# Product order in the gated experts, biases among the sends, linear attention in two phases, and routers' normalisations without turned tokens

## The reference, cut to what matters

```python
# the mixtures of experts (L0, L1, L3, each used twice): a router picks 2 of 8 experts (L1: 1, by capacity)
logits = x @ router_w.T (+ router_b)            # [4096, 8]
# L3 has gated experts with biases
h1, h2 = split(x @ w1[e].T + b1[e], 2)          # 2 x 512
out_e  = (silu(h1) * h2) @ w2[e].T + b2[e]
y      = sum over the 2 chosen e of weight_e * out_e

# L0_attn_b, linear attention, 16 heads of 8, two key/value sets
q, k_i = unit(silu(x @ Wq) + 0.5), unit(silu(x @ Wk[i]) + 0.5)   # unit: divided by each head's norm
state  = product over i of (k_i.T @ v_i / SEQ), per head
y      = (groupnorm(q @ state) * g + b) @ Wo + bo
```

## Time and profile before

| | us |
|---|---|
| median of 3 runs (lowest, highest) | 6225.26 (6223.73, 6227.15) |
| the profiled execution's own time | 6223.72 |
| its span | 6221.8 |
| PE / PEld / DVE busy | 3906.2 (63%) / 2459.3 (40%) / 3758.3 (60%) |
| ACT / POOL busy | 2448.4 (39%) / 1708.2 (27%) |

### The profile page before, as it was taken

One profiled execution on the slowest core, in us unless ns is written; L12 is line 12 of the kernel. 1 busy time (PEld: TensorE's weight loads), 2 busy tenths in 40 slices (PEclk: granted clock), 3 DMA queues, 4 the chain that ended last, 5 costly groups with the idle time before them and its releaser, 6 DMA issues. The chain is left out here.

```text
span 6221.8 us, 78605 instructions
## 1 busy us (share of the span) xinstructions
PE 3906.2 (63%) x21844; PEld 2459.3 (40%) x21844; DVE 3758.3 (60%) x6990; ACT 2448.4 (39%) x4474; POOL 1708.2 (27%) x1709
## 2 busy tenths in 40 slices
PE   5756648466664488724666664688855847476474
PEld 3546438222233233322222223344434636454464
DVE  4323651599974677544888886655567635566354
ACT  2334226355532277613545443233333524243242
POOL 0043014355542355422333340000001140301412
PEclk8868659688876699856778785799966779887898
DMA  2012003100001222012000000000000011100111
GB/s 82 0 55 75 1 10 91 41 1 0 0 4 54 74 82 89 22 36 79 0 1 0 0 0 2 18 1 0 0 2 2 2 45 41 39 8 2 45 42 51
DMA packets 224866, 170.50 MB, mean 27 GB/s; under 512 B 27435, under 2 KB 211602, under 8 KB 223714
## 3 DMA queue, kind: packets, MB, share of 16 engines
q1 hardware_dynamic: 204130, 125.44, 6.8%
q0 software_dynamic: 20480, 41.98, 2.3%
HBM read 92.02 MB, written 74.45 MB: 27 GB/s over the span
## 5 line engine op out<-in xcount | busy, mean ns | idle before, releaser
L1775 POOL TENSOR_TENSOR XN<-s_l_attn_a_h,LOG 128x512 f32<-128x512 f32 x512 | 642.5, 1276 | 768.6 <-DVE s_l_attn_a_h L1815 753.5
L1815 DVE TENSOR_TENSOR_SCAN s_l_attn_a_h<-s_l_attn_a_da,XN 128x512 f32<-128x512 f32 x512 | 598.5, 1211 | 142.9 <-ACT s_l_attn_a_da L1760 102.7
L1751 PE MATMUL s_l_attn_a_y_ps<-XN,c_ident 128*128 128x512 f32 x1024 | 588.7, 704 | 25.2 <-DVE s_l_attn_a_y L2027 15.4
L1760 ACT ACTIVATE s_l_attn_a_da<-s_l_attn_a_delta,s_l_attn_a_a 128x510 f32<-128x510 f32 x512 | 353.3, 690 | 526.0 <-DVE s_l_attn_a_h L1815 525.5
L483 DVE COPY s_l_ffn_ffn_xt<-s_l_ffn_ffn_turned 128x128 f32<-128x128 f32 x416 | 120.9, 292 | 711.1 <-PE s_l_ffn_ffn_turned L604 709.5
L569 POOL DMA_INDIRECT s_l_ffn_ffn_back<-slots_y,s_l_ffn_ffn_slots x320 | 302.8, 946 | 875.3 <-DMA slots_y<-PICK 566.4
L623 PE MATMUL s_l_ffn_ffn_down<-down,s_l_ffn_ffn_hid 128*128 x2944 | 421.1, 284 | 193.4 <-DVE s_l_ffn_ffn_hid L496 186.0
L623 PEld LDWEIGHTS s_l_ffn_ffn_down<-down,s_l_ffn_ffn_hid 128*128 128x128 f32 x2944 | 361.2, 192 | 233.6 <-issue 228.5
L416 ACT COPY s_l_ffn_ffn_own_w<-up 128x512 f32 (+2 forms) x416 | 305.0, 734 | 375.4 <-DVE s_l_ffn_ffn_expert_no L467 277.3
L1730 PE MATMUL s_l_attn_a_spread<-s_l_attn_a_parts,s_l_attn_a_pick 96*128 96x512 bf16 x512 | 182.2, 443 | 390.3 <-DVE XN L1806 243.2
L561 POOL DMA_INDIRECT slots_x<-XN,s_l_ffn_ffn_slots x320 | 311.5, 973 | 388.9 <-DVE s_l_ffn_ffn_slots L460 293.2
(11 more groups left out here) (631 smaller groups left out, 8651.3 us busy)
## 6 DMA issues: line engine op xcount, KB each, us to landing
XNT<-slots_x SPq DMA_DIRECT2D x32, 640.0 KB, 6.3
slots_y<-LOG SPq DMA_DIRECT2D x16, 640.0 KB, 4.3
slots_y<-PICK SPq DMA_DIRECT2D x16, 640.0 KB, 4.3
s_l_attn_b_qr<-s_l_attn_b_q_rows SPq DMA_DIRECT2D x64, 144.0 KB
s_l_attn_b_kr<-s_l_attn_b_k_rows SPq DMA_DIRECT2D x64, 144.0 KB
XNT<-slots_x SPq DMA_DIRECT2D x8, 768.0 KB, 7.0
slots_x<-PICK SPq DMA_DIRECT2D x10, 512.0 KB, 6.4
slots_x<-XN,s_l_ffn_ffn_slots POOLq DMA_INDIRECT x320, 2.2
```

The lines of the kernel that those rows point to most:

```text
L1751: last = self.nc.tensor.matmul(self.y_ps[:, i, :], self.k.ident[:], self.hc[n % 2][:, i, :], start=(n == 0), stop=(n == NST - 1))
L1760: self.nc.scalar.activation(self.da[:, i, :, 1:], self.delta[par][:, i, :].rearrange("p (b t) -> p b t", b=BPG)[:, :, 1:], ACT.Exp, scale= ...
L1775: self.nc.gpsimd.tensor_tensor(self.hc[n % 2][:, i, :], self.h[n % 2][:, i, :], self.c_rows[n % 2], ALU.mult).then_inc(self.hc_ready, 1)
L1815: self.nc.vector.tensor_tensor_scan(self.h[n % 2][:, i, :], self.da[:, i, :, :].rearrange("p b t -> p (b t)"), self.u[n % 2][:, i, :], 0.0 ...
```

## The change

Four edits, in the order of the file.

1. `layer_norm` gets `keep_cols`. The six normalisations of routers pass False: ScalarE then writes only `cols`, and TensorE waits for that copy on `turned_free`.
2. In `sparse_experts`, where gated, the work of `expert_bias` (which is gone) joins the block: GpSimd's product first of all, TensorE's turns and products between the ranks and the experts, VectorE's adds behind the gates. The four PSUM buffers of the up products serve for it; `ranks` shares two of them, hence `slots_used`.
3. In the loop over tiles, `gate_hid(j - 1)` stands ahead of `shift(j)`.
4. `l0_attn_b` runs in two phases: a turn of the loop does the first half (projection to state) of one pair of units and the second half (q times state to x) of the pair before. The projections of both units share one set of PSUM banks. It takes no statistics any more, so the next normalisation does.

```diff
@@ layer_norm
-                        pe.wait_ge(cols_ready, g + (i + 1))
+                        if keep_cols:
+                            pe.wait_ge(cols_ready, g + (i + 1))
+                        else:
+                            pe.wait_ge(turned_free, g + (i + 3))
...
-                        nc.scalar.copy(cols[i][:], turned[i][:]).then_inc(cols_ready, 1)
-                    nc.scalar.copy(xnt, turned[i][:]).then_inc(turned_free, 1)
+                        copied = nc.scalar.copy(cols[i][:], turned[i][:])
+                        copied.then_inc(cols_ready if keep_cols else turned_free, 1)
+                    if keep_cols:
+                        nc.scalar.copy(xnt, turned[i][:]).then_inc(turned_free, 1)
@@ sparse_experts, vector
+            if gated:
+                dve.sem_inc(slots_used, 1)
...
             dve.drain()
+            if gated:
+                for g in range(GROUPS):
+                    dve.wait_ge(bias_up, g + 1)
+                    xg = k.X[:, g * GT:(g + 1) * GT, :]
+                    nc.vector.tensor_tensor(xg, xg, bias_ps[g % 4], ALU.add).then_inc(bias_added, 1)
+                dve.drain()
             for j in range(min(2, NT)):
                 take_xt(j)
             for j in range(NT):
                 if j + 2 < NT:
                     take_xt(j + 2)
                 if gated:
-                    shift(j)
                     if j > 0:
                         gate_hid(j - 1)
+                    shift(j)
@@ sparse_experts, scalar
+                act.wait_ge(gates_up, 1)
+                for h in range(2):
+                    last = nc.scalar.copy(gates_t[:, h, :], turned[h][:])
+                last.then_inc(gates_turned, 1)
@@ sparse_experts, gpsimd
+            if gated:
+                nc.gpsimd.tensor_tensor(spread[:],
...
+                                        ALU.mult).then_inc(spread_ready, 1)
             pool.wait_ge(slots_ready, 1)
@@ sparse_experts, tensor, behind the ranks
+                for h in range(2):
+                    last = nc.tensor.transpose(turned[h][:], k.GATE[:, h * HT:(h + 1) * HT, :].rearrange("p t e -> p (t e)"), k.ident[:])
+                last.then_inc(gates_up, 1)
+                pe.wait_ge(gates_turned, 1)
+                pe.wait_ge(spread_ready, 1)
+                pe.wait_ge(slots_used, 1)
+                for g in range(GROUPS):
+                    if g >= 4:
+                        pe.wait_ge(bias_added, g - 3)
+                    h, q = divmod(g * GT, HT)
+                    nc.tensor.matmul(bias_ps[g % 4], gates_t[:, h, :], spread[:, q:q + GT, :], start=True, stop=True).then_inc(bias_up, 1)
+                pe.wait_ge(bias_added, GROUPS)
             pe.wait_ge(experts_ready, 1)
@@ l0_attn_b
-        proj = s.two_ps("proj", [P, TPB, 4 * D])
+        proj, proj_v = s.ps("proj", [P, TPB, 4 * D]), s.ps("proj_v", [P, TPB, 2 * D])
...
+            step(0, None)
+            with engine.Fori(0, PAIRS - 1) as pair:
+                step(pair * 2 + 2, pair * 2)
+            step(None, BATCH - 2)
...
+            # tensor, step(a, b): a is the newer pair, b the older
+                if a is not None:
+                    project(a, 0)
+                if b is not None:
+                    take_from_state(b, 0)
+                    take_from_state(b + 1, 1)
+                if a is not None:
+                    project(a + 1, 1)
+                if b is not None:
+                    turn_out(b, 0)
+                    turn_out(b + 1, 1)
+                    project_out(b, 0)
+                    project_out(b + 1, 1)
+                if a is not None:
+                    turn_and_add_up(a, 0)
+                    turn_and_add_up(a + 1, 1)
```

More of the change, by code:

```diff
@@ L649, in l0_ffn @@
         consts, loads = sparse_consts(nc, k, s)
-        layer_norm(nc, k, name + "_ln", k.bufs["L0_ffn_router"], 8, keep_rows=True, loads=loads)
+        layer_norm(nc, k, name + "_ln", k.bufs["L0_ffn_router"], 8, keep_rows=True, loads=loads, keep_cols=False)
         softmax8(nc, k, name + "_gate", False)
         sparse_experts(nc, k, name + "_ffn", consts, 2, 4, 4)
[L655 to L699, removed]
@@ L1006, in l0_attn_b @@
     HD = 8
-    BPG = 1
+    PAIRS = BATCH // 2
     with Scope(nc, name) as s:
@@ new lines, in project, with take_from_state @@
+            def project(u, m):
+                pe.wait_ge(xg_ready, u + 1)
+                since(pe, biased, u)
+                for t in range(TPB):
+                    xt = xg[m][:, t * P:(t + 1) * P]
+                    nc.tensor.matmul(proj[:, t, :], xt, w["L0b_w"][:, 0:4 * D], start=True, stop=True)
+                    last = nc.tensor.matmul(proj_v[:, t, 0:D], xt, w["L0b_w"][:, 4 * D:5 * D], start=True, stop=True)
+                last.then_inc(projected, 1)
+            def take_from_state(u, m):
+                pe.wait_ge(done, u + 1)
+                pe.wait_ge(state_ready, u + 1)
+                pe.wait_ge(qt_ready, u + 1)
+                for t in range(TPB):
+                    last = nc.tensor.matmul(o_ps[m][:, t, :], qt[m][:, t * P:(t + 1) * P], state[m][:], start=True, stop=True)
+                last.then_inc(o_ready, 1)
@@ new lines, in turn_and_add_up @@
+            def turn_and_add_up(u, m):
+                pe.wait_ge(unit, u + 1)
+                for t in range(TPB):
+                    last = nc.tensor.transpose(turned_q_ps[m][:, t * P:(t + 1) * P], a[m][:, t, 0:D], k.ident[:])
+                last.then_inc(turned_q, 1)
+                for i in range(2):
+                    for t in range(TPB):
+                        last = nc.tensor.matmul(st_ps[m][:, i, :], a[m][:, t, (1 + i) * D:(2 + i) * D], z[m][:, t, (3 + i) * D:(4 + i) * D],
+                                                start=(t == 0), stop=(t == TPB - 1))
+                last.then_inc(stated, 1)
@@ new lines, in keep_qt, with keep_out, step @@
+            def keep_qt(u, m):
+                act.wait_ge(turned_q, u + 1)
+                nc.scalar.copy(qt[m][:], turned_q_ps[m]).then_inc(qt_ready, 1)
+            def keep_out(u, m):
+                act.wait_ge(turned_o, u + 1)
+                nc.scalar.activation(ont[m][:], turned_o_ps[m], ACT.Identity, bias=w["L0b_be"][:], scale=w["L0b_g"][:]).then_inc(ont_ready, 1)
+            def step(a, b):
+                if a is not None:
+                    keep_x(a, 0)
+                    keep_x(a + 1, 1)
+                    activate(a, 0)
+                    activate(a + 1, 1)
+                if b is not None:
+                    keep_out(b, 0)
+                    keep_out(b + 1, 1)
+                if a is not None:
+                    roots(a, 0)
+                    roots(a + 1, 1)
+                    keep_qt(a, 0)
+                    keep_qt(a + 1, 1)
@@ new lines, in step @@
+            def step(a, b):
+                if a is not None:
+                    add_bias(a, 0)
+                if b is not None:
+                    variance(b, 0)
+                    variance(b + 1, 1)
+                if a is not None:
+                    add_bias(a + 1, 1)
+                if b is not None:
+                    normalise(b, 0)
+                    normalise(b + 1, 1)
+                if a is not None:
+                    square(a, 0)
+                    square(a + 1, 1)
+                    scale(a, 0)
+                    scale(a + 1, 1)
+                if b is not None:
+                    add_out(b, 0)
+                    add_out(b + 1, 1)
+                if a is not None:
+                    mask_state(a, 0)
+                    mask_state(a + 1, 1)
@@ L1180, in l3_attn_b @@
+            over_phases(dve, step)
 def l3_attn_b(nc, k, name):
```

218 lines of the change are left out of this document (88 added, 130 removed).

## The result

The changed kernel takes 5956.5 us (median of four runs, 5949.3 to 5958.7) against 6224.5 for the kernel before: ratio 0.9569, 95% interval 0.9552 to 0.9585, 268 us less. The forecast of 5990 was 34 us too high, inside its range (5950 to 6060) near the lower end. The profiled execution took 5949.3 (span 5947.4, before 6221.8: 274.4 less).

A forecast was written before the change was run, and what follows sets the result against it. In the gated loop TensorE idles 186.0 us waiting for `hid`, TensorE and VectorE working in alternation. Terms -184 - 24 - 27 = -235, taken from the median 6225.3, give 5990 us (chance 0.62); range 5950 to 6060 for 8 in 10.

The forecast's parts named there:

- Gated loop: Gated experts' tile loop: product ahead of the next biases cuts a tile from 4.17 to 2.92 us; -184 for two layers.
- I take 3.05 us a tile: Gated loop from tile 48 of 80 on, where VectorE also combines returned rows: 3.05 us a tile, 3.45 at the upper bound.
- Biases among the sends: Gated experts, gates to sends: the last biases lose their own block and run among the sends; -24 for two layers.
- I take 1.0: Sends of a gated layer: slowed by VectorE's eight bias adds beside them, 1.0 us, from a span of 0 to 1.8.
- I take 0.4: Rank chain ahead of the sends: slowed by POOL's spread product, 0.4 us, from a span of 0 to 3.6.
- Linear attention: Linear attention in two phases: output product's wait goes, the projection becomes late next; -27, bounds 9 to 38 us saved.
- Period 16.8 + 2.0 + 4.2 = 23.0: Linear attention, us per pair: VectorE's work 16.8, small gaps 2.0, idle for state and projection 4.2; 27.9 before.
- Routers' normalisations: Routers' normalisations: one ScalarE copy of 0.59 us per group less, hidden by TensorE's loads; 0, at best 7 us saved.
- A: Rival, gated loop: the value load waits for the product, 3.21 and 3.45 us a tile, total 6042; chance 0.20.
- B: Rival, linear attention: projection at half clock is late in every step, -9 in place of -27, total 6008; chance 0.12.
- C: Rival, gated loop: TensorE put to 1.2 GHz once busy throughout, 5.5 us a tile, 6406 if all are so; chance 0.03.
- D: Rival, gated loop: the product's new place does nothing since TensorE did not wait for `hid`, total 6174; chance 0.03.

The follow-up runs named there:

- the sequential form: The changed kernel with the linear attention's two phases not overlapped, each pair's two half steps before the next pair; ratio 0.9709 against the kernel before.
- the last four runs: Changed kernel with: linear attention not overlapped, 0.9709; expert number read ahead of xt copy, 0.9572; that plus one down product less, 0.9561; that read plus statistics in linear attention, 0.9579.

## Why the prediction was right, and where by luck

**What bounds the kernel** was read rightly: the wait for `hid` and its cause, two engines in alternation. The order alone gave 205 us.

**Gated loop, -184, measured -203 in the traces.** The mechanism and the steady tile (2.82) were right to the hundredth, and so was the claim that loads and loop are level. Three sizes were off; the numbers are those of the first layer. "I take 3.05 us a tile" with combines: it is 2.93 over the last 31, since combine and statistics fall almost wholly into the time in which VectorE waits for silu. Without combines the mean is 2.88, forecast 2.92. That they are near is in part luck: 2.92 stood for two chains that wait a little for each other, but the undisturbed tiles take 2.82, and the mean is above it because of slow tiles of 3.2 to 3.4 us. The trace before has such tiles too (4.8 us in place of 4.17), and without the last three steps its mean is 4.24, not the 4.17 of the forecast: some 5 us more to gain. The "less 4 for the first and last tiles" did come: the last three steps took 6.76 us before, shorter than any other three, and take 8.49 after, so 1.7 us are lost there.

**Biases among the sends, -24, by the traces -24.** The right sum is luck in part: two wrong terms offset each other. Gates to mask fell by 13.5 (forecast 13.4). "I take 1.0" for slower sends: the 32 starts span 39.74 us, before 39.64, so 0.1. "I take 0.4" for the rank chain: 1.5. I had thought only of the spread. TensorE idled 14.6 us ahead of the rank products, no longer 1.6 (the block with its products had been in front), and they run at the lower of its two clocks. The windows of the rank products, after and then before:

```profile
4931.60:4933.90 2.30, 2.16 (x6) 1.63 (x6) 0.00 (x1) 0.00 (x0) 2.30 (x1) 0.50 0.00 0
...
5001.00:5002.20 1.20, 1.10 (x4) 0.68 (x4) 0.00 (x0) 0.00 (x0) 0.00 (x0) 1.00 0.00 0
```

That is 0.9 of the 1.5. The same products of the ungated layers, which have no such block in front, took 1.19 and 1.06 us in the trace before already, behind 10.4 to 15.0 us of idling. Another 0.26 is one instruction: `reach`, both inputs in SBUF, took 0.69 beside the spread and 0.43 before, in both gated layers. The rest, 0.3, is a gap marked "issue" ahead of `base`; the second gated layer has none, and its way grew by 1.2 only. The lock of the Trainium skill (SBUF — State Buffer, Who interferes with whom) is seen in part: the one such instruction that met the spread took longer, yet it had started 0.41 before the spread ended, and the chain lost 0.26 and not 3.6: for most of the spread's time it waited for TensorE anyway. The adds, with an input in PSUM, cost the sends nothing, as the same page has it.

**Linear attention, -27, measured -43.** The step that was mis-sized is "Period 16.8 + 2.0 + 4.2 = 23.0"; it is 20.5. VectorE's work is 16.2 (99.61 us in 126/20.5 = 6.15 periods), not 16.8. The small gaps are about 1.1, not 2.0. The idle time for state and projection is (7.5 + 14.6)/7 = 3.2, not 4.2: I had put the projection between its prices at full and at half clock, and it ran at full clock (granted 1.00 from 703 to 706 us), 1.02 us for two products of 512 columns, right behind the state products. The three make 0.6 + 0.9 + 1.0 = 2.5. My own sum with 20.5 in it gives 7 x 7.4 + 1 - 2 - 6.3 = 44.5; with the mean period before, 27.5, it gives 42. The mechanism (the output wait goes, the projection is late next) was right, and the sequential form shows it from the other side.

**Routers' normalisations, 0:** right.

**The rivals.** A (the read serialises, 3.21 us a tile): no; the read behind a product that had to wait costs 0.22 in a steady tile. Its price of 0.55 and more is seen only about once in ten tiles, where a gap marked "issue" of 0.65 to 0.73 stands ahead of shifted_b; the kernel before has slow tiles at the same places, with 1.2 in place of 0.55 (last section). B: no, by the period. C: the clock in the gated loop is 1.00. D: no, by the order alone.

**Sum.** By the traces -203 - 24 - 43 = -270, and their spans differ by 274.4; the medians differ by 268. The other 4 us lie between steps that the change does not touch and that scatter both ways: one attention step takes 551.1 us in the trace before and 544.5 in the one after, another 246.2 and 254.6. The forecast's 235 fell short by 19 us in the gated loops and 16 in the linear attention.

## What to carry to other kernels

When two engines alternate, write down both cycles in full after the change: their lengths here met within 0.03 us, and from then on only shortening both moves anything. A scalar read is an instruction in its engine's queue: in front of a product that others wait for it cost 10 us a layer, behind it or ahead of an idle stretch little or nothing. Taking out a block also takes out what kept TensorE busy in front of the next products; price these at the low clock.

## What was not expected of the hardware

TensorE's granted clock was 0.50 in the rank products after 14.6 us of idling and 1.00 after 1.6; 1.19 and 1.06 us against 0.67 and 0.59.

The slow tile once in ten stands behind the moment at which SP issues the store of ten results and, 0.47 us later, the load of the next ten tiles, in the kernel after and in the kernel before:

```profile
5027.47 0.62 SPq L609 DMA_DIRECT2D XNT<-slots_x  x1
5031.04 0.69 DVE L503 TENSOR_TENSOR s_l_ffn_ffn_shifted_b<-s_l_ffn_ffn_up_b,L_ffn_b 128x512 f32<-128x512 f32 x1 [0.66 <-issue]
...
5106.65 0.62 SPq L581 DMA_DIRECT2D XNT<-slots_x  x1
5108.87 0.69 DVE L491 TENSOR_TENSOR s_l_ffn_ffn_shifted_b<-s_l_ffn_ffn_up_b,L_ffn_b 128x512 f32<-128x512 f32 x1 [1.21 <-issue]
```

In the first gated layer after the change the first five of these loads each have a gap of 0.65 to 0.73 us ahead of the shifted_b that starts 3.6 to 3.7 us behind them; before the change it was 2.2 us behind. Around the one shown, ScalarE and TensorE have gaps of 0.50 and 0.53 marked "issue" too. That the slow tile mostly vanishes when VectorE's read has idle time in front of it suggests that the read is what comes late on VectorE; why it does, and what the transfers have to do with it, is not shown.

On the chip of the last four runs the kernel before took 6401.5 us, not 6229, and in the four traces there the first two gated products stood 26.0 to 27.4 us apart (2.8 to 3.2 elsewhere after the change), in one of them with TensorE's up products starting one by one 0.7 to 2.8 us apart behind gaps marked "issue". What the engines waited for stays open.
